# Eight experts written out one by one in a mixture-of-experts stage, with the splitting of their weights shared out over three engines

## The chip, the cores and the metric

One core of one Trainium2 chip. The metric is the device time of one execution in microseconds; engines are TensorE (PE in the profile, its weight loads PEld), VectorE (DVE), ScalarE (ACT), GpSimd (POOL) and SyncE (SP, which here only issues DMAs). T stands for the start of a tile's first matmul where a schedule is worked out.

## The reference, cut to what matters

`x` is 2 x 1024 tokens of 256 features. Two attention layers and a small MLP over the context come first and don't change. Then a top-1 mixture of experts, with 8 experts and a hidden size of 1024:

```python
x = x + _L1_ffn_ref(_layernorm(x), w_router, w1, b1, w2, b2)
# in it:
probs = softmax(x @ w_router); sel = argmax(probs); wgt = probs[sel]
for e in range(8):
    h = relu(xt @ w1[e] + b1[e])          # 256 -> 1024
    y = h @ w2[e] + b2[e]                 # 1024 -> 256
    out = out + ((sel == e) * wgt)[:, None] * y
```

## The kernel before

The program is a row of blocks with a barrier of all engines between them. The last two matter here: `context_mlp` (span 451 to 531 us), which ends with the routing, and `experts` (531 us to the end).

**Routing.** `context_mlp` normalises the rows, computes the router's logits, and gives each token a slot: the tokens of an expert fill tiles of 128 slots, and each expert's first slot starts a new tile. `steps` decides how many tiles an expert has: its first entry is -1, so that an expert has at least one tile, even with no token. `MT` = 23 is the most tiles there can be; how many there are (`TILES`) is known only on the chip. `table` holds for each tile its expert, then for each tile whether it exists, then where each expert's tiles end. Rows go to DRAM (`rows`, with mean and 1/std beside them), and POOL fetches the rows of a tile by an indirect DMA (`gather`) to `xg`.

**Weights.** Matmuls run in fp32r. For precision each fp32 operand is split into a rounded high part and the rest: `wh` and `wl` for weights, `xh`/`xl` and `hh`/`hl` for the two layers' inputs, and each product is three matmuls (high x high, low x high, high x low). Raw weights of an expert (`wst`, 2 MB with both layers) and a bias row come by DMA from SP; all three have two buffers, by `e % 2`. Experts 0 and 1 are fetched in `context_mlp`. There ACT makes the high parts of both (8 copies, L1234), and POOL the low parts of expert 0 (`low(0)` to `low(3)`, L1662); the low parts of expert 1 are POOL's at the start of `experts`. For every later expert POOL makes both parts, in three pairs (L1501 high, L1504 low: two halves of the first layer at 1024 columns, then the second layer at 2048), when the first tile of the expert before it begins. SP fetches an expert's weights when the low parts of expert e-2 are done (`next_expert`).

**A tile.** `tiles` runs `body(0)` and then a loop on every engine over the tiles from 1 to `TILES`, with the tile's expert read from `table` into a register and all weight and bias addresses computed from it. In the order of each queue, for tile g:
- PE: `hidden(g)` (L1615, 12 matmuls of 512 columns), `transpose_x(g+1)` (L1604), `output(g-1)` (L1634, 24 matmuls of 256 columns), `transpose_h(g)` (L1624, 8 transposes).
- DVE: `e_h` (L1583, bias added, two halves), `x_low(g+1)` (L1562), `finish(g-1)` (L1568 `e_y`, then L1571, which adds the weighted result to the row in `xg`), `e_hl` (L1591, two halves), `normalise(g+2)` (L1557).
- ACT: `x_high(g+1)` (L1536), relu to `e_hh` (L1545, two halves).
- POOL, written out for every g up to `MT` with conditions from `table`: gather of tile g+3 (L1668), the next expert's split where a new expert begins, and the scatter of tile g-1 to the output (L1527). Reads of `table` into registers are at L1471.

`e_y` of tile g is computed while tile g+1 is under way, and PE's `output(g)` stands behind `hidden(g+1)` in its queue.

Of the kernel before, what the change touches and what calls it, by code (L numbers as in the profile page):

```python
# [10 lines left out]
ALU = mybir.AluOpType  # L11
# [26 lines left out]
ROW = D + 2  # L38
MT = B * S // P + NE - 1
TG = MT + 2  # L40
TABLE = 2 * TG + NE + 1
TILES, LAST = 2 * TG + NE - 1, 2 * TG + NE
# [1069 lines left out]
def context_mlp(nc, top, t, io):  # L1112


    with ExitStack() as ctx:
# [3 lines left out]
        def sem(name):  # L1119
# [7 lines left out]
        mv4, rstd4 = x_all[:, :, D:D + 2], x_all[:, :, D + 1]  # L1127
# [21 lines left out]
        w_high = t["w_high"] = sem("c_w_high")  # L1149
# [11 lines left out]
                 "inner_s", "th_s", "g_s", "o_ps", "x_done", "r_ps", "shift", "exp", "oh_s", "count_ps", "sent_s", "here_s", "inv_ps", "src_s")  # L1161
        (dve, pool_sem, consts, var_ready, rstd_ready, xn_ready, xT_ps, xT_sb, h_ps, sq_ready, inner_ready,
         th_ready, g_ready, o_ps, x_done, r_ps, shifted, exp_done, oh_ready, count_ps, sent_ready, here_ready, inv_ps, src_ready) = (
# [3 lines left out]
        @block.sync  # L1167
        def _(sp):
            fetch_expert(sp, t, io, 0)
            sp.wait_ge(t["w_in"], 48)  # L1170
            fetch_expert(sp, t, io, 1)
            rows = t["rows"].rearrange("(t p) r -> p t r", p=P)
            for n in range(NC):
                sp.wait_ge(rstd_ready, n + 1)
                sp.dma_start(rows[:, n * CH:(n + 1) * CH], x_all[:, n * CH:(n + 1) * CH]).then_inc(stored, 16)
            next_expert(sp, t, io, 2)

        @block.gpsimd
        def _(pool):
# [18 lines left out]
            def low(i):  # L1198
                split_low(pool, t, w_high, i)

            power(0)
            low(0)
            power(1)
            low(1)
            power(2)
            power(3)
            low(2)
            low(3)
# [5 lines left out]
        def _(act):  # L1214
# [15 lines left out]
            def high(i):  # L1230
                x, q = divmod(i, NC)
                act.wait_ge(t["w_in"], 48 * (x + 1))
                part = quarter(q)
                act.copy(t["wh"][:, x, part], t["wst"][:, x, part]).then_inc(w_high, 1)  # L1234

# [4 lines left out]
            for n in range(1, NC):  # L1240
# [3 lines left out]
                if n >= 2:  # L1244
                    high(n - 2)
            copy_x(NC + 1)
            high(2)
            copy_x(NC + 2)
            high(3)
            copy_x(NC + 3)  # L1250
            high(4)
            high(5)
            act.wait_ge(shifted, 1)
            act.activation(e[:], e[:], ACT.Exp).then_inc(exp_done, 1)
            high(6)
            high(7)

        @block.vector
        def _(vec):
            link = Link(vec, dve)  # L1260

            def normalise(i):
# [10 lines left out]
                ins.then_inc(xn_ready, 1)  # L1273

# [35 lines left out]
            vec.memset(steps[:, 0:1], -1.0)  # L1310
# [123 lines left out]
def experts(nc, top, t, io):  # L1434

    with ExitStack() as ctx:
# [3 lines left out]
        def sem(name):  # L1440
# [3 lines left out]
        bias = t["bias"]  # L1444
# [5 lines left out]
        dst, share, landed = t["dst"], t["share"], t["landed"]  # L1450
# [4 lines left out]
        names = ("dve", "xn_s", "xT_ps", "xh_s", "xl_s", "h_ps", "h_sb", "hT_ps", "hh_s", "hl_s",  # L1455
                 "y_ps", "y_s", "y_done", "out_s", "hgone")
        (dve, xn_ready, xT_ps, xh_ready, xl_ready, h_ps, h_sb, hT_ps, hh_ready, hl_ready, y_ps, y_sb,
         y_done, out_done, hgone) = (sem("e_" + n) for n in names)
        w_high = [sem(f"e_w_high{i}") for i in range(3)]
        w_in, w1_ready, w_ready = t["w_in"], t["w1_ready"], t["w_ready"]  # L1460
# [9 lines left out]
        def load(eng, at, top_value, least=0):  # L1470
            return eng.value_load(table[0:1, bass.ds(at, 1)], min_val=least, max_val=top_value)  # L1471

        def tiles(eng, body):

            body(0)
            with eng.Fori(1, load(eng, TILES, MT, NE)) as g:
                body(g)

        @block.sync
        def _(sp):  # L1480
            for e in range(3, NE):
                next_expert(sp, t, io, e)
            written = sp.to_reg(load(sp, TILES, MT, NE) * 16)
# [4 lines left out]
        def _(pool):  # L1488
            most = pool.to_reg(B * S - 1)

            def split(g, e, par):
                fetched = pool.to_reg(e * 48 + 96)
                pool.wait_ge(h_ps, 2 * g)
                pool.wait_ge(w_in, fetched)
                for part in range(3):
                    raw, high, low = (
# [265 lines left out]
```

## Time and profile before

| | us |
|---|---|
| median of 3 runs | 744.81 |
| the three runs | 745.09, 744.81, 739.28 |
| the profiled execution: its time | 744.16 |
| its span in the trace | 742.4 |
| mean granted TensorE clock over the span | 0.895 of full |
| PE, DVE, ACT, POOL busy | 599.1, 498.7, 292.4, 321.5 |

The span is what the trace covers; the 1.76 us between it and the execution's time lie around it. Busy time is summed over the whole program, of which the experts stage is the last 211 us. A granted clock of 1.0 is 2.4 GHz and 0.5 is 1.2 GHz. In a row, "x12" is the number of instructions, and a bracket at the end says how long the engine sat idle before it and what released it.

### The profile page before, as it was taken

The numbers are of one execution on the slowest core, as the hardware profiler recorded it, in microseconds if no ns is written. First come the engines' busy times: TensorE is split into PE (matmuls) and PEld (weight loads), VectorE is DVE, ScalarE is ACT, GpSimd is POOL, SyncE is SP. The second block draws the span as 40 slices with busy tenths as digits, with TensorE's granted clock in tenths as the row PEclk, the third lists the DMA queues.
The fourth block names the chain that finished last, engine by engine and source line by source line (L and its number), as shares of the span: only waits on it lengthen the run. The fifth ranks groups of instructions, "written<-read, shape, count | busy, mean of one in ns | idle before, by whom it ended". The sixth has DMA issues, their size and how long they took to land. (4 is left out here: it accounts for less than half of the span.)

```text
span 742.4 us, 12123 instructions
## 1 busy us (share of the span) xinstructions
PE 599.1 (81%) x3667; PEld 521.3 (70%) x3668; DVE 498.7 (67%) x950; ACT 292.4 (39%) x536; POOL 321.5 (43%) x271
## 2 busy tenths in 40 slices
PE   4588999953579999999999985675668959687984
PEld 4467888953468888888888872465557847576874
DVE  4698888855027888889889864774376636536562
ACT  1144554512146878778788701332012102111210
POOL 3344434421413344344344311250166956697265
PEclk9799999995699999999999997955579989988997
DMA  6111111100344232322322005323032451422110
GB/s 211 29 45 42 30 28 29 29 9 0 90 112 86 47 81 44 83 47 57 72 45 43 0 1 193 134 87 149 20 121 73 156 182 36 174 101 84 43 28 18
DMA packets 24823, 53.10 MB, mean 72 GB/s; under 512 B 4570, under 2 KB 11483, under 8 KB 22730
## 3 DMA queue, kind: packets, MB, share of 16 engines
q1 hardware_dynamic: 20474, 45.10, 20.6%
q0 software_dynamic: 2208, 5.41, 2.6%
q10 hardware_dynamic: 2096, 2.05, 0.9%
q8 instruction: 21, 0.34, 0.2%
q14 instruction: 24, 0.20, 0.1%
HBM read 31.55 MB, written 4.87 MB: 49 GB/s over the span
## 5 line engine op out<-in xcount | busy, mean ns | idle before, releaser
L881 POOL TENSOR_SCALAR h_p<-h_p,h_rs 128x1024 f32<-128x1024 f32 x64 | 72.5, 1132 | 131.5 <-DVE h_rs L973 131.5
L980 DVE TENSOR_REDUCE h_nmx<-h_psS 128x1 f32<-128x1024 f32 x64 | 78.1, 1221 | 22.4 <-PE h_psS L1071 21.0
L960 DVE TENSOR_TENSOR h_pTl<-h_psT,h_pTh 128x512 fp32r<-128x512 f32 x128 | 81.5, 678 | 4.4 <-ACT h_pTh L908 4.4
L908 ACT CAST h_pTh<-h_psT 128x512 fp32r<-128x512 f32 x128 | 69.2, 590 | 29.6 <-PE h_psT L1031 29.6
L930 ACT ACTIVATE h_p<-h_psS,h_nmx 128x1024 f32<-128x1024 f32 x64 | 72.3, 1129 | 17.7 <-DVE h_nmx L980 17.7
L1042 PE MATMUL h_psO<-h_pTh,h_vs 128*128 128x256 f32 x256 | 70.0, 307 | 3.1 <-DVE h_oT L968 2.3
L308 POOL TENSOR_TENSOR a_p<-a_p,a_rs 128x616 f32<-128x616 f32 x32 | 39.0, 1220 | 73.9 <-DVE a_rs L355 73.9
L1031 PE MATMUL h_psT<-ident,h_p 128*128 128x128 f32 x512 | 67.4, 273 | 1.4 <-DVE h_pTl L960 1.2
L1031 PEld LDWEIGHTS h_psT<-ident,h_p 128*128 128x128 f32 x512 | 59.1, 141 | 11.2 <-issue 3.3
L1042 PE MATMUL h_psO<-h_pTl,h_vs 128*128 128x256 f32 x256 | 63.8, 282 | 0.0
L1504 POOL TENSOR_TENSOR wl<-wst,wh 128x1024 fp32r<-128x1024 f32 (+1 forms) x18 | 56.0, 3114 | 2.7
L1071 PE MATMUL h_psS<-h_kh,h_qs 128*128 128x512 f32 x128 | 56.0, 438 | 0.7 <-DMA h_kl<-h_lo 0.7
L1536 ACT CAST e_xh<-e_psX 128x256 fp32r<-128x256 f32 x22 | 8.2, 374 | 119.3 <-PE e_psX L1604 119.3
L1615 PE MATMUL e_psH<-wh,e_xh 128*128 (+1 forms) x84 | 37.8, 450 | 21.4 <-POOL wl L1504 12.5
L1634 PE MATMUL e_psY<-wh,e_hh 128*128 (+1 forms) x168 | 52.7, 314 | 2.5 <-DVE e_hl L1591 2.5
L1042 PEld LDWEIGHTS h_psO<-h_pTh,h_vs 128*128 128x128 f32 x256 | 48.5, 190 | 7.2 <-issue 5.6
L1071 PE MATMUL h_psS<-h_kl,h_qs 128*128 128x512 f32 x128 | 50.9, 397 | 0.0
L1634 PE MATMUL e_psY<-wh,e_hl 128*128 (+1 forms) x168 | 50.4, 300 | 0.0
L1634 PE MATMUL e_psY<-wl,e_hh 128*128 (+1 forms) x168 | 50.3, 299 | 0.0
L1668 POOL DMA_INDIRECT xg<-rows,src x25 | 26.0, 1038 | 54.6 <-DVE src L1352 27.0
L1042 PEld LDWEIGHTS h_psO<-h_pTl,h_vs 128*128 128x128 f32 x256 | 48.8, 191 | 0.3
L1545 ACT ACTIVATE e_hh<-e_psT 128x512 fp32r<-128x512 f32 x42 | 22.9, 595 | 63.8 <-PE e_psT L1624 63.6
(262 smaller groups left out, 1506.3 us busy)
## 6 DMA issues: line engine op xcount, KB each, us to landing
wst<-in_m_w SPq DMA_DIRECT2D x16, 1024.0 KB, 5.9
bias<-in_m_b SPq DMA_DIRECT2D x8, 640.0 KB, 8.6
h_kh<-h_hi SPq DMA_DIRECT2D x32, 128.0 KB, 2.4
h_kl<-h_lo SPq DMA_DIRECT2D x32, 128.0 KB, 2.4
rows<-x_all SPq DMA_DIRECT2D x4, 516.0 KB, 3.4
a_qs<-a_qhi SPq DMA_DIRECT2D x16, 128.0 KB, 2.3
a_qs<-a_qlo SPq DMA_DIRECT2D x16, 128.0 KB, 2.3
h_qs<-h_hi SPq DMA_DIRECT2D x16, 128.0 KB, 2.2
```

The lines of the kernel that those rows point to most:

```text
L308: pool.tensor_tensor(p3, p3, rs[:, u, :].unsqueeze(2).to_broadcast([P, HH, L]), ALU.mult).then_inc(pn_ready, 1)
L881: pool.tensor_scalar(pr[:, u % 4], pr[:, u % 4], rs[:, u:u + 1], 0.0, ALU.mult, ALU.add).then_inc(pn_ready, 1)
L908: act.copy(pTh[u // QP % 2][:, hf * HK:(hf + 1) * HK, u % QP * P:(u % QP + 1) * P], psT[hf][:]).then_inc(pT_hi, 1)
L930: act.activation(pr[:, u % 4], psS[u % 2][:], ACT.Exp, bias=nmx[:, u:u + 1], scale=1.0, accum_out=sm[:, u:u + 1]).then_inc(exp_done, 1)
L960: vec.tensor_tensor(pTl[u // QP % 2][part], psT[hf][:], pTh[u // QP % 2][part], ALU.subtract).then_inc(pT_lo, 1)
L980: vec.tensor_reduce(nmx[:, u:u + 1], psS[u % 2][:], AX.X, ALU.max, negate=True).then_inc(max_ready, 1)
L1031: ins = pe.transpose(psT[hf][:, k], pr[:, u % 4, (hf * HK + k) * P:(hf * HK + k + 1) * P], ident[:])
L1042: ins = pe.matmul(psO[:, 0:QP * P], vs[i % 2][:, k], part[g % 2][:, k], start=(k == 0 and part is pTh), stop=(k == KT - 1 and part is pTl))
L1071: ins = pe.matmul(psS[u % 2][:, hf * CW:(hf + 1) * CW], qs[i % 2][:, q * P:(q + 1) * P], part[i % 2][:, hf * CW:(hf + 1) * CW], start=(par ...
L1504: pool.tensor_tensor(low, raw, high, ALU.subtract).then_inc((w1_ready, w1_ready, w_ready)[part], 1)
L1615: ins = pe.matmul(psH[hf][:], x_[:, k], w_[:].rearrange("p a w -> p (a w)")[:, bass.ds(off, 512)], start=(k == 0 and n == 0), stop=(k == K ...
L1634: ins = pe.matmul(psY[:, 0:D], h_[:, k], w_[:].rearrange("p a w -> p (a w)")[:, bass.ds(off, D)], start=(k == 0 and n == 0), stop=(k == FB ...
```

## The change

- `steps` gets a second entry of -1: every expert has at least two tiles. `MT` becomes 30, `TG` 32.
- `tiles` is written out for the 8 experts: for each a `body` for its first tile and a loop over its others, whose ends are read from `table`. Weight and bias addresses are constants; only the tile's number is a register.
- ACT makes all high parts, in an expert's first tile: the second layer's of this expert (`high2`, two copies) before `x_high(g+1)`, and the first layer's of the next expert (`split_high`, two copies) after it. DVE makes the second layer's low parts of this expert (two subtractions of 1024 columns) between `x_low(g+1)` and `finish(g-1)`. POOL makes the first layer's low parts of the next expert (two subtractions of 1024 columns).
- In `context_mlp` only the first layer of expert 0 is split. SP fetches first-layer weights with the biases, and second-layer weights, apart from each other.
- `normalise` moves from DVE to ACT, as an activation with a scale and a bias per row; `rows` carries -mean/std for it as a third extra column (`ROW` = 259), four small DVE instructions in `context_mlp`.
- Rows are fetched 4 tiles ahead; POOL's gather moves behind the split and into the condition that the tile exists.
- PE waits for both halves of `h_sb` and of `hl` where it waited for one.

The diff, cut to its core:

```diff
-MT = B * S // P + NE - 1
+MT = B * S // P + 2 * (NE - 1)
...
-            vec.memset(steps[:, 0:1], -1.0)
+            vec.memset(steps[:, 0:2], -1.0)
...
             power(0)
-            low(0)
+            split_low(pool, t, 0, 0)
             power(1)
-            low(1)
+            split_low(pool, t, 0, 1)
             power(2)
             power(3)
-            low(2)
-            low(3)
...
         def tiles(eng, body):
-            body(0)
-            with eng.Fori(1, load(eng, TILES, MT, NE)) as g:
-                body(g)
+            for e in range(NE):
+                first = load(eng, ENDS + e - 1, MT - 2 * (NE - e), 2 * e) if e else 0
+                body(first, e, True)
+                with eng.Fori(first + 1, load(eng, ENDS + e, MT - 2 * (NE - 1 - e), 2 * e + 2)) as g:
+                    body(g, e, False)
...
         def _(sp):
-            for e in range(3, NE):
-                next_expert(sp, t, io, e)
+            for e in range(2, NE):
+                sp.wait_ge(low1, 2 * (e - 1))
+                if e >= NB:
+                    sp.wait_ge(bias_free, e - NB + 1)
+                fetch_first(sp, t, io, e)
+                sp.wait_ge(low2, 2 * (e - 1))
+                fetch_second(sp, t, io, e)
...
+            def split(e, par):
+                for hf in range(2):
                     pool.wait_ge(landed, 16)
+                    pool.wait_ge(high1, pool.to_reg(e * 2 + (hf + 3)))
+                    raw, high, low = (halves(w, 1 - par)[:, :, hf] for w in (wst, wh, wl))
+                    pool.tensor_tensor(low, raw, high, ALU.subtract).then_inc(low1, 1)
...
                 with pool.If(load(pool, TG + g - 1, MT) > g - 1):
+                    if g + 4 < TG:
+                        pool.wait_ge(landed, 16 * (g + 4))
+                        gather(pool, t, g + 4)
                     pool.wait_ge(y_done, g)
...
         def _(act):
+            def normalise(g):
+                upto(act, xT_ps, g, 1, 0)
+                upto(act, landed, g, 16, 16)
+                row = xg[:, bass.ds(g, 1), :].rearrange("p a r -> p (a r)")
+                act.activation(xn[:], row[:, 0:D], ACT.Identity, bias=row[:, D + 2:D + 3],
+                               scale=row[:, D + 1:D + 2]).then_inc(xn_ready, 1)
...
+            def body(g, e, first):
+                if first:
+                    for x in range(2):
+                        act.wait_ge(t["in2"][e % 2], 16 * (e // 2 + 1))
+                        act.copy(second(wh, e, x), second(wst, e, x)).then_inc(high2, 1)
                 x_high(g + 1)
+                normalise(g + 2)
+                if first and e + 1 < NE:
+                    split_high(act, t, e + 1, 0)
+                    split_high(act, t, e + 1, 1)
...
         def _(vec):
...
                 x_low(g + 1)
-                if not isinstance(g, int):
-                    finish(g - 1)
+                if first:
+                    for x in range(2):
+                        vec.wait_ge(high2, 2 * e + x + 1)
+                        vec.tensor_tensor(second(wl, e, x), second(wst, e, x), second(wh, e, x),
+                                          ALU.subtract).then_inc(low2, 1)
+                if not first:
+                    finish(g - 1, e)
+                elif e:
+                    finish(g - 1, e - 1)
+                    vec.sem_inc(bias_free, 1)
```

## Rows read from the trace of the kernel before

**Rows 1.** One line's instructions: how often, ns min/median/max, first and last start

```profile
L1568 DVE TENSOR_TENSOR e_y<-e_psY,bias x21: 424/425/426, 556.6 to 735.1; 128x256 f32<-128x256 f32 x21
```

**Rows 2.** Who waited for whom, 530 to 742.4 us: us in total, times, longest

```profile
PE e_psX L1604 <- DVE e_xn L1557: 20.0, 5, 7.7
...
DVE e_xn L1557 <- DMA xg<-rows,src: 12.6, 4, 7.5
```

**Rows 3.** Timeline of POOL, the first instruction of each split; then all scatters of one line

```profile
567.47 1.05 POOL L1501 TENSOR_SCALAR wh<-wst 128x1024 fp32r<-128x1024 f32 x1 [0.47 <-PE e_psH L1615]
...
583.85 1.06 POOL L1501 TENSOR_SCALAR wh<-wst 128x1024 fp32r<-128x1024 f32 x1
...
623.66 1.05 POOL L1501 TENSOR_SCALAR wh<-wst 128x1024 fp32r<-128x1024 f32 x1 [0.40 <-PE e_psH L1615]
...
648.20 1.05 POOL L1501 TENSOR_SCALAR wh<-wst 128x1024 fp32r<-128x1024 f32 x1 [1.06 <-issue]
...
664.45 1.07 POOL L1501 TENSOR_SCALAR wh<-wst 128x1024 fp32r<-128x1024 f32 x1
...
715.00 1.05 POOL L1501 TENSOR_SCALAR wh<-wst 128x1024 fp32r<-128x1024 f32 x1 [0.45 <-PE e_psH L1615]
...
L1527 POOL DMA_INDIRECT out<-xg,dst x21: 1006/1012/1052, 558.0 to 736.6; - x21
```

**Rows 4.** Timeline of all engines, one tile without a split

```profile
556.98 0.48 PE L1615 MATMUL e_psH<-wh,e_xh 128*128 x1
...
559.99 0.36 PE L1634 MATMUL e_psY<-wh,e_hh 128*128 x1
...
560.35 0.37 ACT L1536 CAST e_xh<-e_psX 128x256 fp32r<-128x256 f32 x1 [2.44 <-PE e_psX L1604]
...
562.88 1.04 PE L1624 MATMUL e_psT<-ident,e_h 128*128 128x128 f32 x8
563.28 0.42 DVE L1568 TENSOR_TENSOR e_y<-e_psY,bias 128x256 f32<-128x256 f32 x1 [1.93 <-PE e_psY L1634]
...
564.28 1.28 DVE L1591 SCALAR_TENSOR_TENSOR e_hl<-e_psT,e_hh 128x512 fp32r<-128x512 f32 x2
...
564.40 0.49 PE L1615 MATMUL e_psH<-wh,e_xh 128*128 x1 [0.48 <-issue]
```

**Rows 5.** Timeline around the last split in context_mlp

```profile
496.15 5.45 DVE L1271 TENSOR_SCALAR xg<-x_all 128x256 f32<-128x256 f32 x4 [1.12 <-POOL x_all L1195]
...
501.65 1.97 PE L1376 MATMUL c_psX<-ident,xg 128*128 128x128 f32 x8 [2.44 <-DVE xg L1271]
```

**Rows 6.** Timeline of the first tiles in experts

```profile
540.93 9.30 POOL L1662 TENSOR_TENSOR wl<-wst,wh 128x1024 fp32r<-128x1024 f32 x4
541.62 8.77 DVE L1557 TENSOR_SCALAR e_xn<-xg 128x256 f32<-128x256 f32 x1
542.64 0.28 PEld L1615 LDWEIGHTS e_psH<-wh,e_xh 128*128 128x128 f32 x1 [2.53 <-issue]
```

**Rows 7.** The row update in DVE, and the nearest instructions for the new ones

```profile
L1571 DVE SCALAR_TENSOR_TENSOR xg<-e_y,share,xg x21: 483/1030/2379, 557.2 to 735.7; 128x256 f32 x21
...
L1234 ACT CAST wh<-wst x8: 1027/1043/1049, 475.7 to 513.3; 128x1024 fp32r<-128x1024 f32 x8
...
L1286 DVE SCALAR_TENSOR_TENSOR x_all<-c_psO,x_all 128x1024 f32<-128x1024 f32 x4 | 4.9, 1216 | 0.0
```

**Rows 8.** Timeline of PE: idle times and the matmuls behind them

```profile
574.73 0.49 PE L1615 MATMUL e_psH<-wh,e_xh 128*128 x1 [1.56 <-POOL wl L1504]
...
683.41 0.69 PE L1604 MATMUL e_psX<-ident,e_xn 128*128 128x128 f32 x2 [3.41 <-DVE e_xn L1557]
689.14 1.12 PE L1624 MATMUL e_psT<-ident,e_h 128*128 128x128 f32 x8
...
730.30 0.58 PE L1634 MATMUL e_psY<-wh,e_hh 128*128 128x256 f32 x1 [2.46 <-DVE e_hl L1591]
```

**Rows 9.** Reads of the table into registers by POOL's sequencer

```profile
L1471 POOLq TENSOR_LOAD <-table x70: 282/289/508, 543.3 to 737.7; - x70
```

More of the change, by code:

```diff
@@ L1638, in _, with body, halves, second @@
             transpose_x(0)
-            def body(g):
-                e = 0 if isinstance(g, int) else load(pe, g, NE - 1)
-                before = 0 if isinstance(g, int) else load(pe, g - 1, NE - 1)
+            def body(g, e, first):
                 hidden(g, e)
                 transpose_x(g + 1)
-                if not isinstance(g, int):
-                    output(g - 1, before)
+                if not first:
+                    output(g - 1, e)
+                elif e:
+                    output(g - 1, e - 1)
                 transpose_h(g)
             tiles(pe, body)
-            output(load(pe, LAST, MT - 1, NE - 1), NE - 1)
-def quarter(q):
-    return slice(q * WE // NC, (q + 1) * WE // NC)
-def split_low(pool, t, w_high, i):
-    x, q = divmod(i, NC)
-    part = quarter(q)
-    pool.wait_ge(w_high, i + 1)
-    pool.tensor_tensor(t["wl"][:, x, part], t["wst"][:, x, part], t["wh"][:, x, part],
-                       ALU.subtract).then_inc(t[("w_split", "w1_ready", "w_split", "w_ready")[q]], 2 if q == 1 else 1)
+            output(load(pe, LAST, MT - 1, 2 * NE - 1), NE - 1)
+def halves(w, par):
+    return w[:, par, 0:KD * FF].rearrange("p (k h f) -> p k h f", k=KD, h=2)
+def second(w, e, x):
+    half = FB * D // 2
+    return w[:, e % 2, KD * FF + x * half:KD * FF + (x + 1) * half]
+def split_high(act, t, e, hf):
+    act.wait_ge(t["in1"][e % 2], 32 * (e // 2 + 1))
+    act.copy(halves(t["wh"], e % 2)[:, :, hf], halves(t["wst"], e % 2)[:, :, hf]).then_inc(t["high1"], 1)
+def split_low(pool, t, e, hf):
+    pool.wait_ge(t["high1"], 2 * e + hf + 1)
+    pool.tensor_tensor(halves(t["wl"], e % 2)[:, :, hf], halves(t["wst"], e % 2)[:, :, hf],
+                       halves(t["wh"], e % 2)[:, :, hf], ALU.subtract).then_inc(t["low1"], 1)
 def gather(pool, t, g):
@@ L1696, in program @@
         t["src"], t["dst"], t["share"] = sb("src", [P, TG], I32), sb("dst", [P, TG], I32), sb("share", [P, TG])
-        for name in ("c_in", "w_in", "w1_ready", "w_ready", "w_split"):
+        for name in ("c_in", "high1", "low1", "high2", "low2"):
             t[name] = top.enter_context(nc.semaphore(name))
+        for name in ("in1", "in2"):
+            t[name] = [top.enter_context(nc.semaphore(f"{name}_{i}")) for i in range(2)]
         t["rows"] = nc.dram_tensor("rows", (B * S, ROW), F32, kind="Internal").ap()
```

152 lines of the change are left out of this document (59 added, 93 removed).

## The prediction

> **What bounds the kernel now.** I read the stage from its ends inward. First, one line that every tile runs once: `e_y` ran 21 times, from 556.6 to 735.1 us [rows 1], so the stage had 21 tiles, the first result came at 556.6, and the other 20 took 178.5 us, 8.9 each. Second, a tile in which nothing goes wrong [rows 4]: PE goes from `hidden` at 556.98 to the next `hidden` at 564.40, 7.42 us. The reader is to see in it that `hidden` and the transposes of x take 3.01, `output` 2.89 (559.99 to 562.88), and the transposes of h 1.04, which makes 6.94 of work, and somewhat less in truth, since the ends are modelled: the two `e_y` at 556.6 and 563.28 [rows 1, 4] are 6.7 apart. I call it 6.8. The last row says that 0.48 before the next tile was "issue", PE waiting for its own sequencer (branch, two reads of the table, address registers). So PE is the bound of a quiet tile, and 8.9 - 6.8 is what the rest costs. Third, the waits [rows 2]: PE waited 20.0 us for the normalised row, and DVE, which normalises, 12.6 for gathered rows; at other places PE waited for POOL's low weights (1.56 at 574.73 [rows 8] is one). All three go back to POOL, which splits the weights of experts 2 to 7 and is late with its gathers for that. The starts of the splits [rows 3] also give the tiles of each expert: a split begins with the first tile of experts 1 to 6, and POOL's 21 scatters (558.0 to 736.6, the last of these rows), counted between those starts, give 3, 1, 5, 2, 1, 7, 1, 1. Four experts have one tile.
>
> **What the change takes away.** (a) In `context_mlp` four normalising instructions took 5.45 us while POOL ran two low parts, and PE waited 2.44 for them [rows 5]. POOL has nothing to run there now: -2.4. Tables of 32 instead of 25 entries lengthen seven small DVE instructions on the same path by some 0.1 each: +0.8. Together **-1.6**. ACT's copies there were idle time and gain nothing.
> (b) At the start of `experts` one `e_xn` took 8.77 us beside four of POOL's subtractions, and PE had its next `hidden` at 542.64 after 2.53 of "issue" [rows 6]. After the change `hidden(1)` can start near 541 and takes 5.1 at half clock (12 matmuls of 512 columns); low part work for expert 1 hides behind ACT's copies; `hidden(1)` and the transposes of x end near 546.4, where before `e_xn` held them until 541.62 + 8.77 = 550.4; `output(0)` at full clock and the 0.4 to `e_y` make 549.6 of the 556.6 of [rows 1]: **-7.0**. It would be 2.4 less if the clock were still low then.
> (c) The waits of [rows 2] are gone as such: POOL keeps two subtractions of six instructions an expert, `normalise` is no longer on the engine that stalls beside POOL's subtractions, and gathers, 4 ahead, lead by three tiles (some 20 us). The longest wait for a gathered row was 7.5, well inside that; if the lead were lost, the 12.6 of [rows 2] is what it costs. They don't enter the sum, which counts what an interval takes after the change.
>
> **What it adds: tiles.** A minimum of two tiles turns the four single ones into two: 25 tiles, 24 intervals instead of 20. A tile inside a loop has no table read and no address work in PE's queue, so I take 6.85, the 6.8 of work and little else (bounds 6.8 and the 7.42 of [rows 4]). The first tile of an expert and the step into its loop still have one read each: 7.1. With 15 such steps and 9 plain ones: 15 x 7.1 + 9 x 6.85 = 168.2.
>
> **What it adds: a collision.** Take a first tile with T at PE's `hidden`, with the offsets of [rows 4]. ACT copies `high2` at T+0.2 to 2.3 (two of 1.04 [rows 7]), hidden. `x_high` is at T+3.4 to 3.75, `normalise` to 4.2 (no row has it; the bounds are the 0.37 for rounding the same size from PSUM [rows 4] and the 1.04 for four times the size [rows 7], and I take 0.45, near the first), `split_high` to 5.2 and 6.2, all before the relu at 6.6. DVE ends `x_low` near 4.25 and makes two low parts of 1.15 to 1.2 each (no row has a subtraction of this size on DVE; the nearest is 1.22 for 1024 columns [rows 7]): until 6.55. POOL starts its first low part when ACT's first half is there, 5.4, or when DVE lets go, 6.55; a pair takes 4.7 (four took 9.30 [rows 6]), so it holds until 10.1 to 11.3. In this time stands `finish(g-1)`, whose second instruction reads two operands from SBUF: it takes 0.48 alone and up to 2.38 beside POOL [rows 7]. And `e_xn` shows that a waiting DVE doesn't get in between two of POOL's subtractions that stand back to back: 8.77 us over four [rows 6]. So the row update, due at T+6.9, ends at 11.6 (if DVE's second part came first) or 12.2 (if POOL came first), `e_hl` behind it at 12.8 to 13.4, and PE, which wants it for `output(g)` at T+7.1+3.0 = 10.1, waits 2.7 to 3.3. The cover that DVE had, `e_hl` ending 1.6 before its use, is used up. Experts 1 to 6 have it (0 has no `finish` there, 7 no next expert): 6 x 2.9 = **17.4**. Bound below: 0.7 each if DVE gets in after one subtraction.
>
> **And the clock.** After 1.56 us of idle PE's matmuls ran at full speed (0.49 for 512 columns), after 2.46 and 3.41 at half (0.58, 0.69) [rows 8]. Behind the second, transposes of x and `output` took 5.73 (683.41 to 689.14) instead of some 3.1, so +2.6; behind the first, `output` took 4.4 (from 730.30 to 0.4 before the last `e_y` at 735.1 [rows 1]) instead of 2.89, so +1.5. Idle times of 2.7 to 3.3 fall on the wrong side: 1.9 each, as the smaller of the two is the nearer, and eight tenths of the six, 11.4: **9.1**. Bounds 0 and 6 x 2.6 = 15.6.
>
> **The end.** POOL walks through the tiles that don't exist: 2 before, 5 now, with six more reads of the table, each about 0.6 with its register work (0.29 alone [rows 9]). They come after the last scatter. If the core's end waits for POOL's last step all of it counts (+3.6), if for the scatter's completion nothing: **+2.0**.
>
> Sum on the profiled execution, whose span is 742.4: -1.6 - 7.0 + (168.2 + 17.4 + 9.1 - 178.5 = +16.2) + 2.0 = 752.0, with the 1.8 around it **753.8** (744.16 before, which is 0.65 under the median). Without collision and clock it would be 727: the gain of the freed PE pays for four more tiles and leaves 17 us, and the collision is what spends it.
>
> **Rivals.** *The clock stays up* (a gap of 2.7 is nearer to 2.46 than to 3.41, and what ran before 730.30 was itself interrupted): 744.7, no change. *DVE gets in after the first subtraction*: for it, no row update took over 2.38 [rows 7] though POOL's passes from [rows 3] are six instructions long, so DVE did get in where a subtraction was followed by a rounding copy; against it, both places with subtractions back to back [rows 5, 6] held DVE to the end. Its price is 0.7 a time and no clock loss: 753.8 - 26.5 + 4.2 = **731.5**, faster. It decides from whether the row update ends below T+9.
>
> By the Trainium skill, "SBUF — State Buffer", section "SBUF: two separate sides", the port pair is a lock that whichever starts first has for the whole of one instruction, which makes this rival the expected course; by that rule the time would be this rival's 731.5, and the 8.77 us of [rows 6] should have been some 2, which the trace contradicts. The same page says that two SBUF inputs make a DVE instruction contend, so that DVE's own low parts take part in it.
>
> *Entering loops is dear*: the one step into the loop that the trace has cost PE 2.53 us of "issue" at its weight loads [rows 6], against 0.48 between tiles [rows 4]. Eight entries and seven exits at 2.0 more each would be 30; six fall into the wait of the collision, so 18: **772**. Against it: three reads of the table stood in that step, and only one is left.
>
> The Trainium skill, "Runtime: NRT & Kernel Launch", section "Instruction fetch mechanics", says that a branch to code outside the two pages held forces a fetch; eight loops instead of one would give that more chances, which is this rival's case. The trace of before doesn't separate it from the table reads.
>
> **How the numbers follow.** Collision with the clock loss 0.50; clock stays up 0.17; DVE gets in 0.22; dear loops 0.11. The first by itself runs from 746 to 760 (collision 2.7 to 3.3, clock 1.5 to 2.4, end 0 to 3.6). For 8 in 10 the range takes in all of these but half of the dear loops and the lower half of the fast rival's spread: 729 to 766. A change of 1% (737.4 and 752.3 against the median) is what can be told from none here. Faster: the fast rival, 0.22. Slower: two thirds of the first and the last, 0.44. Within: the rest, 0.34.
>
> **What would show it.** `e_y` x25, the first near 548. Quiet intervals of 6.8 to 7.1. In the first tiles of experts 1 to 6 the row update (`finish`) near 4 us or DVE's second low part that long, then PE idle 2.5 to 3.5 for `e_hl` ahead of `output`, and its matmuls at half speed. Right before: no `e_xn` wait, no wait for `wl`. It would be wrong if the stage's first tiles are as short as its others (fast rival), if "issue" before PE's matmuls grows (dear loops), or if gathers or weights come late in spite of (c), for which I have no term.

## The result: slower, 774.5 us

The changed kernel takes 774.5 us (median of 4 runs, 768.2 to 775.5) against 744.95 in the runs beside it, a ratio of 1.040 (95% interval 1.036 to 1.044). Forecast were 753.8 and a range of 729 to 766. The profiled execution has a span of 772.9 against 742.4, so 30.5 us have to be found. Here and below ratios rest on the fast runs alone, those within 1.5% of a kernel's fastest, while medians and ranges take in all runs.

**First the same line as before.** Tile results (`e_y`) and row updates of the kernel after, one line's instructions (how often, ns min/median/max, first and last start):

```profile
L1568 DVE TENSOR_TENSOR e_y<-e_psY,bias x25: 415/424/426, 555.2 to 750.5; 128x256 f32<-128x256 f32 x25
L1570 DVE SCALAR_TENSOR_TENSOR xg<-e_y,share,xg x25: 484/486/2699, 555.9 to 751.1; 128x256 f32 x25
```

Set against [rows 1], there are 25 tiles, as forecast; the first comes 1.4 us earlier, and the 24 intervals take 195.3 instead of 178.5. After the last `e_y` 22.4 us are left, where it was 7.3. The stage's first `e_xn` starts at 536.65 instead of 531.22. So the 30.5 are: context stage and routing +5.4 (0.9 of it arises ahead of the stage, in code that is the same: its first instruction starts at 451.75 instead of 450.88); from there to the first `e_y` -6.8; intervals +16.8; last `e_y` to last scatter +7.1 (8.5 in place of 1.4); last scatter to the end +8.1 (13.9 in place of 5.8).

**Then the waits.** Kernel after, 528 to 773 us (in total, times, longest; the rows that matter here):

```profile
POOL xg L1680 <- issue: 84.3, 24, 7.9
ACT e_xn L1530 <- DMA xg<-rows,src: 52.7, 17, 9.2
PE e_psY L1637 <- DVE e_hl L1596: 11.9, 8, 2.8
PE e_psX L1608 <- ACT e_xn L1530: 9.7, 3, 5.4
PE e_psH L1618 <- POOL wl L1493: 7.3, 4, 3.0
POOL out L1519 <- issue: 7.3, 24, 0.3
```

The wait of `normalise` for gathered rows, 12.6 in [rows 2] and declared gone by my part (c), is now 52.7, in 17 places. And POOL waits for no finished tile any more: before each scatter it sits idle for only 0.3. The scatters start 4.1 to 16.1 us after the row update that they wait for has ended. POOL is the engine that is late.

**What POOL does in a tile.** Timelines of POOL, then of ACT's `normalise`, in a stretch without a split:

```profile
611.37 1.02 POOL L1680 DMA_INDIRECT xg<-rows,src  x1 [7.13 <-issue]
612.69 1.02 POOL L1519 DMA_INDIRECT out<-xg,dst  x1 [0.30 <-issue]
617.11 1.03 POOL L1680 DMA_INDIRECT xg<-rows,src  x1 [3.40 <-issue]
618.44 1.03 POOL L1519 DMA_INDIRECT out<-xg,dst  x1 [0.30 <-issue]
623.22 1.02 POOL L1680 DMA_INDIRECT xg<-rows,src  x1 [3.76 <-issue]
624.55 1.02 POOL L1519 DMA_INDIRECT out<-xg,dst  x1 [0.30 <-issue]
629.87 1.02 POOL L1680 DMA_INDIRECT xg<-rows,src  x1 [4.29 <-issue]
```

```profile
608.71 0.60 ACT L1530 ACTIVATE e_xn<-xg 128x256 f32 x1 [8.22 <-DMA xg<-rows,src]
614.46 0.60 ACT L1530 ACTIVATE e_xn<-xg 128x256 f32 x1 [3.92 <-DMA xg<-rows,src]
620.27 0.60 ACT L1530 ACTIVATE e_xn<-xg 128x256 f32 x1
```

A quiet pass takes 5.7 to 6.7 us from gather to gather: until the gather has landed (2.84 the first time, and the scatter stands inside this time), then three reads of the table with their register work (0.6 to 0.7 each), then 0.7 before the next gather goes out. The row gathered at 611.37 is normalised at 614.46, as soon as it lands, and behind the gather of 617.11 the same 3 us follow. In the whole stage no row is normalised more than 7.6 us after its gather went out. Rows are asked for "4 ahead", yet no lead is left. The reason is a line of the change that my list of it left out, though it is part of the diff, behind each scatter:

```
 pool.indirect_dma_start(out=io["out"], ..., in_=xg[:, g - 1, 0:D], ...).then_inc(out_done, 16)
+pool.wait_ge(landed, 16 * min(g + 5, TG))
```

`gather(g + 4)` is the (g + 5)th, so POOL stands in each pass until the gather that it has just issued has landed. Before, it waited for the gather of the pass before, which had landed beside the wait for the tile. A pass with a split (two subtractions of 4.7 to 4.9 more, and waits around them) takes 10.2 to 12.4. The passes right behind the first four splits are nearly as long, 9.5 to 10.2: the end of a split lets SP fetch another expert's first-layer weights, and the gather that goes out in the same moment lands only after 6.6 (issued at 601.87, landed at 608.46), with POOL waiting for it. TensorE's tile is 6.7 to 7.0, so a quiet pass wins back 1 us at best, and the two passes around such a split lose 6 or more. There was no lead to begin with: gathers 3 and 4 stand behind the split of expert 1, and the first scatter starts 10.8 us after its row update. Even through six quiet tiles on end POOL stays 6.5 to 7.2 behind.

Six of the 24 intervals are over 10 us. Three have a late row in them, the other three POOL's late low parts: PE waited 3.03, 1.99 and 1.83 for these and went on at a granted clock of 0.50 to 0.66. One of each kind:

```profile
609.37 0.44 PE L1608 MATMUL e_psX<-ident,e_xn 128*128 128x128 f32 x2 [1.86 <-ACT e_xn L1530]
...
639.91 0.79 PE L1618 MATMUL e_psH<-wh,e_xh 128*128 128x512 f32 x1 [3.03 <-POOL wl L1493]
```

The chain that ended last, from the profile's page, says the same of the whole execution:

```profile
DMA xg<-rows,src 15%; POOLq L1455 4%; POOL wl L1493 2%; POOL wl L1674 0%; POOL out L1519 0%; POOL xg L1680 0%; POOLq L1514 0%; POOLq L1508 0%; ACT wh L1668 0%; POOLq L1506 0%; POOLq L1680 0%; POOLq L1511 0%; POOLq L1491 0%; ACT e_xn L1530 0%; ACTq L1455 0%
```

15% of 772.9 is 116 us in which the end hung on a gathered row: nothing that an engine computes. Before it was 5%.

**The context stage.** Timeline of DVE, then of POOL, kernel after; these answer to [rows 5]:

```profile
477.37 1.37 DVE L1253 TENSOR_SCALAR xg<-x_all 128x256 f32<-128x256 f32 x4
478.66 2.31 DVE L1258 SCALAR_TENSOR_TENSOR x_all<-x_all 128x4 f32<-128x4 f32 x1
480.89 1.21 DVE L1272 SCALAR_TENSOR_TENSOR x_all<-c_psO,x_all 128x1024 f32<-128x1024 f32 x1
...
491.21 2.31 DVE L1258 SCALAR_TENSOR_TENSOR x_all<-x_all 128x4 f32<-128x4 f32 x1
```

```profile
477.75 3.20 POOL L1674 TENSOR_TENSOR wl<-wst,wh 128x1024 fp32r<-128x1024 f32 x1 [2.32 <-ACT wh L1668]
484.24 1.11 POOL L1194 TENSOR_TENSOR x_all<-x_all,c_mhalf 128x4 f32<-128x4 f32 x1 [3.29 <-DVE x_all L1276]
490.29 3.21 POOL L1674 TENSOR_TENSOR wl<-wst,wh 128x1024 fp32r<-128x1024 f32 x1 [4.94 <-ACT wh L1668]
```

The new shift of four columns, -mean/std, reads two operands from SBUF, and two of the four took 2.31 us, until POOL's low part ended, with the update of `x_all` queued behind them (the other two, with POOL quiet, took 0.16). I had no term for these instructions at all.

**The end.** Reads of the table by POOL from 755 us on, and its last step before the end:

```profile
L1455 POOLq TENSOR_LOAD <-table x11: 283/288/293, 755.3 to 767.5; - x11
...
L1422 POOLq DRAIN  x1: 4484/4484/4484, 768.2 to 768.2; - x1
```

The last scatter, at 759.0, is followed by the wait for a gather, the reads of five tiles that don't exist until 768.2, and a drain of 4.5.

### The profile page after: what moved, and what is told of

It reads as the page before. It is cut to its first block and busy times, and to the rows that moved or that the text cites. A ratio compares the mean times of both kernels' runs of the same rounds, so it can differ in the third digit from the quotient of the medians.

```text
span 772.9 us, 11969 instructions
## 1 busy us (share of the span) xinstructions
PE 626.2 (81%) x3851; PEld 548.7 (71%) x3851; DVE 510.4 (66%) x974; ACT 336.1 (43%) x599; POOL 272.0 (35%) x252
## 5 line engine op out<-in xcount | busy, mean ns | idle before, releaser
L1680 POOL DMA_INDIRECT xg<-rows,src x30 | 32.1, 1069 | 132.4 <-issue 84.3
L1637 PE MATMUL e_psY<-wh,e_hh 128*128 128x256 f32 x200 | 61.2, 306 | 12.0 <-DVE e_hl L1596 11.9
L1637 PE MATMUL e_psY<-wh,e_hl 128*128 128x256 f32 x200 | 58.8, 294 | 0.0
L1637 PE MATMUL e_psY<-wl,e_hh 128*128 128x256 f32 x200 | 58.8, 294 | 0.0
L1618 PE MATMUL e_psH<-wh,e_xh 128*128 128x512 f32 x100 | 44.9, 449 | 9.5 <-POOL wl L1493 7.3
L1581 DVE TENSOR_TENSOR e_h<-e_psH,bias 128x512 f32<-128x512 f32 x50 | 33.7, 688 | 25.5 <-PE e_psH L1618 23.7
L1637 PEld LDWEIGHTS e_psY<-wh,e_hh 128*128 128x128 f32 x200 | 40.4, 202 | 14.1 <-DVE e_hl L1596 14.1
L1530 ACT ACTIVATE e_xn<-xg 128x256 f32 (+1 forms) x27 | 16.2, 602 | 72.5 <-DMA xg<-rows,src 52.7
```

The lines of the kernel that those rows point to most:

```text
L1581: vec.tensor_tensor(h[:, hf], psH[hf][:], b1(e, hf), ALU.add).then_inc(h_sb, 1)
L1618: ins = pe.matmul(psH[hf][:], x_[:, k], halves(w_, e % 2)[:, k, hf], start=(k == 0 and n == 0), stop=(k == KD - 1 and n == 2))
L1637: ins = pe.matmul(psY[:, 0:D], h_[:, k], w_[:, e % 2, at:at + D], start=(k == 0 and n == 0), stop=(k == FB - 1 and n == 2))
```

## The experiments

Each ratio is to the kernel before, run beside it on the same chip; the kernel before has medians of 740.7 to 744.95 on the different chips, so medians of different chips can differ by 4 us for that alone. e1 to e4 share a chip, so do e6 to e9, and e10 to e12.

```
run                   us median (range)        ratio [95%]              tiles  intervals  last scatter to end
after                 774.5 (768.2 to 775.5)   1.040 [1.036, 1.044]     25     195.3      13.9
e1_no_landed          741.4 (733.3 to 750.4)   0.997 [0.994, 1.001]     25     181.8      11.2
e2_shift_last         766.0 (763.2 to 768.2)   1.033 [1.028, 1.038]     25     194.2      14.0
e3_short_tail         756.3 (755.9 to 758.4)   1.020 [1.016, 1.023]     25     185.3       8.4
e4_three              729.5 (725.1 to 732.7)   0.982 [0.976, 0.988]     25     174.1       5.8
e5_before_two_tiles   784.9 (784.0 to 786.2)   1.057 [1.053, 1.060]     25     207.4      18.6
e6_gathers_first      718.3 (711.7 to 725.9)   0.961 [0.956, 0.966]     25     168.3       5.7
e7_split_late         726.4 (725.3 to 727.5)   0.978 [0.974, 0.981]     25     169.9       6.2
e8_all                718.2 (714.6 to 719.0)   0.967 [0.964, 0.971]     25     162.3       6.2
e9_single             711.7 (708.4 to 714.3)   0.958 [0.953, 0.963]     21     158.7       5.2
e10_single_early      701.3 (697.4 to 704.3)   0.945 [0.939, 0.951]     21     147.9       5.0
e11_pieces            722.1 (719.1 to 723.7)   0.974 [0.969, 0.978]     25     164.7       7.8
e12_pieces_single     702.6 (700.4 to 705.6)   0.947 [0.941, 0.952]     21     152.9       5.0
```

**One repair at a time, and together.** First the wait alone:

```
-                    pool.wait_ge(landed, 16 * min(g + 5, TG))
```

> The changed kernel without the one wait that POOL has behind every scatter, for the landing of the gather it has just issued (the gather's own wait for its predecessor stays). Theory A, POOL's serial chain (gather 1.0, landing 2.8 to 7.3, table reads, and the split behind it) is what made rows late (ACT waited 52.7 us for them) and left POOL 8.5 us behind the last row update: 24 intervals shrink from 195.3 to 172 to 185 us and the lag at the end by some 7, so 746 to 760 us. Theory B, as predicted blind, the collision of POOL's subtractions with DVE's row update is the price: the gathers come earlier, nothing else moves, 768 to 776. Theory C, gathers are late because weights are being fetched, not for the order in POOL: half of A's gain, 760 to 768.

Measured: 0.997, 4.3% or some 32 us less than the change, more than any of the three expectations, and level with the kernel before. Waits of e1, 528 to 748 us:

```profile
POOL xg L1679 <- DMA xg<-rows,src: 45.4, 14, 6.3
POOL out L1519 <- DVE xg L1569: 28.8, 11, 3.2
ACT e_xn L1529 <- DMA xg<-rows,src: 18.9, 5, 9.5
```

POOL waits for finished tiles again (28.8, where it was next to nothing), and its scatters start 0.3 to 6.0 us after their row updates, but for the first (10.8). `normalise` waits for rows in 5 places instead of 17, four of them among the first tiles. The trace is of an execution of 750.4 us, 9 above the median, so its parts add to 24 only: intervals 13.5, the lag behind the last `e_y` 7.1, the end 2.7, the first `e_y` 0.9. Theory C has a share in the mechanism: a gather beside a fetch of weights still takes 6.6 to land here, only nothing stands still for it any more. This one line is the difference between a change that costs 30 us and one that costs nothing.

Second, the shift in one instruction of 16 columns after the last `normalise`, with one wait for it in SP:

```
-                if i >= NC:
-                    part = slice(n * CH, (n + 1) * CH)
-                    vec.scalar_tensor_tensor(shift4[:, part], mv4[:, part, 0], ...).then_inc(shift_ready, 1)
+                if i == 2 * NC - 1:
+                    vec.scalar_tensor_tensor(shift4, mv4[:, :, 0], ...).then_inc(shift_ready, 1)
```

> The changed kernel with the four 128x4 instructions that make -mean/std in context_mlp put into one 128x16 behind the last normalising, so that the four stores of rows wait for it. Theory A, two of the four (2.31 us each where 0.16 is the bare cost) stood behind POOL's subtractions and delayed the stage: the stage is 4.3 us shorter, 769 to 771 us. Rival, the delay was hidden by PE or the stores become late instead (they take 4 us each and the first gather waits for them at 532): 773 to 776.

Measured: 766.0 us, less than was expected, and the first `e_y` at 546.3, 9.0 earlier; the new instruction, no longer beside POOL, takes 0.18:

```profile
L1257 DVE SCALAR_TENSOR_TENSOR x_all<-x_all x1: 183/183/183, 495.8 to 495.8; 128x16 f32<-128x16 f32 x1
```

Of the 9.0, 2.0 arise ahead of the stage, in code that is the same (its first instruction starts at 449.76 instead of 451.75). So the shifts cost 7.0: 4.3 are the two holds, and 2.6 a wait of DVE for ACT's tanh behind the first (4.11 instead of 1.49). Without them the stage gained 2.5 on the kernel before, where I forecast 1.6. In the ratio 0.7% came of it (some 5 us).

Third, POOL's conditions for tiles 17 on nested in each other, so that the first tile that doesn't exist skips the rest; tiles 1 to 16, which always exist, lose their condition and its table read:

```
-                with pool.If(load(pool, TG + g - 1, MT) > g - 1):
+            for g in range(1, 2 * NE + 1):
+                tile(g)
+            with ExitStack() as rest:
+                for g in range(2 * NE + 1, MT + 1):
+                    rest.enter_context(pool.If(load(pool, TG + g - 1, MT) > g - 1))
+                    tile(g)
```

> The changed kernel with POOL's conditions for tiles 17 to 30 nested in each other, so that after the last live tile it reads the table once instead of nine times. Theory A, the core's end waits for POOL's last step and then its drain: 9.2 us from the last scatter to the drain become 2.5 to 3, so 767 to 769 us. Rival, the drain waits for the last scatter's own completion (it took 4.5 us after the dead tiles): the drain grows by what the steps lose, 772 to 775.

Measured: 2.0% less than the change (15 us, twice what was expected). The end took 8.4 in place of 13.9; the rest came in the intervals, 185.3 in place of 195.3. The landed wait is still in this kernel, and one table read less (0.29 in each pass, and what goes with it) paid because POOL's pass set the pace. POOL's drain stayed as it was (4.56, 4.48 in the change), so the rival is out.

> All three edits together. If they are independent (theory A each): 774.5 less 14 to 28, less 4.3, less 6.5, so 736 to 750 us. If the collision that was predicted blind only appears once POOL is on time (its subtractions then begin at T+5.4 to 6.5 of an expert's first tile and the row update stands at T+6.9), the trace shows row updates of 4 to 5 us for experts 1 to 6, PE idle of 2.5 to 3.5 behind each, and the time is at the upper end or over it, 745 to 755.

All three together: 0.982, 1.8% faster than before, and 729.5 us is under both expectations. The gains alone add to 4.3 + 0.7 + 2.0 = 7.0 points, together they give 5.8; the first and the third shorten the same passes, though with the intervals of the four ratios the difference isn't far from noise. What is left shows in the intervals: 22 of 24 are 5.6 to 7.8, and two are 11.6 and 12.1.

**The price of the tiles by itself.** The kernel before with only the minimum of two:

```
-MT = B * S // P + NE - 1
+MT = B * S // P + 2 * (NE - 1)
-            vec.memset(steps[:, 0:1], -1.0)
+            vec.memset(steps[:, 0:2], -1.0)
```

> The kernel before with only the minimum of two tiles for each expert (25 tiles in place of 21; nothing else of the change). It prices the added tiles alone. Theory: four more intervals of about 7 us, and fewer weight stalls since experts of one tile are gone (the two intervals of 17 us of before shrink): 24 intervals of 186 to 200 us against 178.5, total 10 to 26 us slower, ratio 1.014 to 1.035. Rival, by which the tiles cost their whole count and nothing is given back: 4 x 8.9 = 36 us slower, ratio 1.048. Rival, by which the old stalls were worth the added tiles: within 5 us, ratio 0.995 to 1.007.

Measured: +5.7%, 42 us, above all three expectations. Timeline of POOL at its end:

```profile
765.84 1.01 POOL L1527 DMA_INDIRECT out<-xg,dst  x1 [3.35 <-DVE xg L1571]
767.15 1.02 POOL L1668 DMA_INDIRECT xg<-rows,src  x1 [0.31 <-issue]
771.53 1.00 POOL L1668 DMA_INDIRECT xg<-rows,src  x1 [3.36 <-DMA xg<-rows,src]
775.93 1.00 POOL L1668 DMA_INDIRECT xg<-rows,src  x1 [3.40 <-DMA xg<-rows,src]
```

28.9 are the intervals, 7.2 a tile that was added. 12.7 are the end: the old loop gathers outside the condition, and 25 tiles with room for 30 leave three gathers of rows of tiles that don't exist, 4.4 each, behind the last scatter. The changed kernel has its gathers inside the condition. So the minimum of two costs the old kernel 42, of which the changed one has only the tiles to pay; how its 30 split into tiles and the rest can't be had by subtracting the two.

**The first tiles.** e4 had one interval of 11.6, with ACT 9.6 in wait for a row until 553.3: gather 3 was queued behind POOL's subtractions for expert 1, and POOL had waited 5.8 for gather 1, beside a weight fetch. e6 is e4 with

```
-            for g in range(1, 3):
+            for g in range(1, 5):
                 pool.wait_ge(landed, 16 * g)
                 gather(pool, t, g)
             split_low(pool, t, 1, 0)
             split_low(pool, t, 1, 1)
-            for g in range(3, 5): ...
```

and the fetch of expert 2's first layer at the end of `context_mlp` instead of at the start of `experts`.

> The kernel with all three repairs (e4), plus gathers 1 to 4 issued ahead of POOL's subtraction pair for expert 1, and the fetch of expert 2's first layer issued at the end of the context stage instead of at the experts' start. Theory: the first tiles of e4 waited for rows only because gather 1 took 5.1 us beside that fetch and gather 3 was issued behind the subtractions of 4.7 us (ACT's normalise waited 9.6 us for it). Then the first interval falls from 11.6 to about 7.2, gather 1 lands in 3 us, and the kernel is 3 to 8 us faster than e4: ratio 0.971 to 0.978 against e4's 0.982. Rival: the four gathers in a row push expert 1's low parts behind the point where TensorE wants them, and the stall only moves to interval 2 or 3: no gain, ratio 0.980 to 0.984.

Measured: 0.961, more than expected (2.2 points under e4, though the ratio rests on few runs and the range is wide). The first interval is 6.8, the first `e_y` at 544.1 (548.9 in e4): the theory held, the rival didn't.

**The collision of my forecast.** In e4 it is there once, whole. Timelines of DVE, POOL and PE:

```profile
581.41 0.42 DVE L1570 TENSOR_TENSOR e_y<-e_psY,bias 128x256 f32<-128x256 f32 x1
582.02 5.58 DVE L1572 SCALAR_TENSOR_TENSOR xg<-e_y,share,xg 128x256 f32 x1 [0.19 <-DVE e_y L1570]
587.52 1.27 DVE L1598 SCALAR_TENSOR_TENSOR e_hl<-e_psT,e_hh 128x512 fp32r<-128x512 f32 x2
...
593.49 0.42 DVE L1570 TENSOR_TENSOR e_y<-e_psY,bias 128x256 f32<-128x256 f32 x1 [3.17 <-PE e_psY L1639]
```

```profile
581.56 1.02 POOL L1516 DMA_INDIRECT out<-xg,dst  x1 [0.30 <-issue]
582.60 4.71 POOL L1492 TENSOR_TENSOR wl<-wst,wh 128x1024 fp32r<-128x1024 f32 x2
```

```profile
588.85 0.39 PE L1639 MATMUL e_psY<-wh,e_hh 128*128 128x256 f32 x1 [3.85 <-DVE e_hl L1598]
```

The row update is held through both subtractions, `e_hl` stands behind it, PE idles 3.85 us, and `output` then takes 4.6 to `e_y` (588.85 to 593.49). In e6 it came once too, in another place; PE idled 3.74, `output` took 4.66 from 626.99 to 631.65, and the granted clock of that stretch was 0.72 of full speed:

```profile
core 0: us, PE busy (x) PEld busy (x) DVE busy (x) ACT busy (x) POOL busy (x), PEclk, DMA share, GB/s
...
619.00:626.00 7.00, 4.25 (x26) 3.44 (x24) 6.80 (x4) 2.49 (x5) 6.82 (x4) 1.00 0.56 187
626.00:632.00 6.00, 5.01 (x30) 5.01 (x31) 2.81 (x6) 0.00 (x0) 1.68 (x2) 0.72 0.86 326
```

e7 is e4 with the two subtractions moved behind the scatter, which waits for the row update (so the gather, too, goes out ahead of them):

```
+                pool.indirect_dma_start(out=io["out"], ...).then_inc(out_done, 16)
                 if g < MT:
                     e = load(pool, g, NE - 1)
                     ... split(e, par)
-                pool.indirect_dma_start(out=io["out"], ...).then_inc(out_done, 16)
```

> The kernel with all three repairs (e4), plus POOL's two subtractions of an expert moved behind the scatter of the same pass, so that they start after VectorE's row update has been made. Theory (my forecast's own collision): the one interval of 12.1 in e4 with its row update of 5.58 us comes from the update falling beside POOL's pair and from the clock lost after it; it goes to about 7.0, and no row update is longer than 2.4: 4 to 6 us faster than e4, ratio 0.974 to 0.977. Rival: the collision moves to another VectorE operation (a low part, 2.35 us the pair) or the late low parts hold TensorE or the next fetch: same as e4 or up to 6 us slower, ratio 0.981 to 0.990.

Measured: no row update over 2.61, and behind the first interval (13.2 here, 11.6 in e4) none over 8.9, so 24 take 169.9 instead of 174.1. The ratio, 0.978, is lower than e4's 0.982, but the intervals overlap: the mechanism is shown in the trace, its price in the time isn't told from none.

> The changes of e6 and of e7 together. If both theories hold the gains add, as they lie in different intervals: 718 to 723 on the scale on which e4 ran 729.5, ratio 0.966 to 0.973, 24 intervals of 163 to 166 us. If one of the two only moves its stall, it shows here as in that run.

Measured: 0.967, and the fewest us for 24 intervals, 162.3, 6.8 each. But it isn't under e6: the medians are the same (718.2 and 718.3), and the intervals of the ratios overlap. The collision is rare enough in e6 that removing it doesn't show in the time.

In e11 each subtraction of e6 is four:

```
-                    pool.tensor_tensor(low, raw, high, ALU.subtract).then_inc(low1, 1)
+                    for k in range(KD):
+                        for c in range(2):
+                            cut = slice(c * 256, (c + 1) * 256)
+                            ins = pool.tensor_tensor(low[:, k, cut], raw[:, k, cut], high[:, k, cut], ALU.subtract)
+                    ins.then_inc(low1, 1)
```

> The kernel of e6 with each of POOL's two subtractions of 128x1024 written as four of 128x256, at the same place. Theory: VectorE is let in between two POOL instructions, and what holds its row update is one instruction's length (2.36 us for a whole one); then no row update is longer than about 1.3 us, the interval of 11.9 is gone and 24 intervals take 163 to 165 in place of 168.3. Total 0 to 6 us less than e6: ratio 0.953 to 0.962. Rival, by which POOL once started keeps VectorE out until it pauses: with no pause between the pieces a row update of 5 us and an interval of 12 still appear, and POOL's pieces cost 0.1 to 0.3 us more each: ratio 0.960 to 0.968.

Measured: in the six places no row update took over 1.05 us (the theory said 1.3), and no interval is over 8.5. Yet the kernel isn't faster than e6. By its ratio, 0.974, it is slower, beyond the rival's figure as well; but its range (719.1 to 723.7) lies inside that of e6 (711.7 to 725.9). POOL's eight pieces take 5.61 instead of 4.7 (timeline of POOL and of DVE):

```profile
571.94 1.03 POOL L1520 DMA_INDIRECT out<-xg,dst  x1 [0.30 <-issue]
573.00 5.61 POOL L1498 TENSOR_TENSOR wl<-wst,wh 128x256 fp32r<-128x256 f32 x8
```

```profile
578.12 0.78 DVE L1576 SCALAR_TENSOR_TENSOR xg<-e_y,share,xg 128x256 f32 x1 [0.20 <-DVE e_y L1574]
```

What the pieces do to the hold is shown; whether the kernel is slower for them isn't (the spans of the two traces are 717.3 and 719.5, the other way round, and e6 wasn't run on the chip of e11).

**One tile again.** e9 is e8, and e10 is e6, with a minimum of one tile and each loop behind a branch:

```
-                with eng.Fori(first + 1, load(eng, ENDS + e, ...)) as g:
-                    body(g, e, False)
+                second_ = first + 1
+                last = load(eng, ENDS + e, ...)
+                with eng.If(last > second_):
+                    with eng.Fori(second_, last) as g:
+                        body(g, e, False)
```

> The kernel of e8 with a minimum of one tile for each expert again, each loop behind a branch that skips it where the expert has a single tile (21 tiles in place of 25). Theory: every tile costs a full interval of 6.7 to 7.0 whatever rows it holds, so four fewer give 26 to 28 us less than e8: ratio 0.930 to 0.937, near 692 to 697. Rival: experts of a single tile leave no quiet interval to round and split the next weights in, so the stalls of weights come back (9 to 17 us intervals as in the kernel before), and half of it is given back: ratio 0.945 to 0.955.

> The kernel of e6 (POOL's subtractions ahead of the gather) with a minimum of one tile, as e9 is that of e8. Theory: in e9 each stall of 15 us was TensorE waiting 5 to 7 us for POOL's low part of the first layer, which was queued behind the wait for the finished tile; issued ahead of it they come some 3 us earlier: three intervals of 11 to 12 in place of 15, 6 to 10 us less than e9: ratio 0.945 to 0.950. Rival: a single tile is too short for fetch, ACT's rounding and POOL's subtraction in a row wherever they stand; same stalls, ratio 0.955 to 0.960.

Measured: e9 0.958, only 7 us under e8, above even its rival's figure. Three intervals are 14 to 15.4 (PE, timeline):

```profile
563.93 0.79 PE L1623 MATMUL e_psH<-wh,e_xh 128*128 128x512 f32 x1 [5.42 <-POOL wl L1498]
```

e10, with the subtractions ahead of the gather, has 9.9, 12.1 and 10.8 there and comes to 0.945: 701.3 us, the fastest of all. So the theory of e10 held: half of the stall was the place of the subtractions, the other half stays. In the new order four tiles more cost 1.5% (e6 against e10) by the ratios, 3 us each, and 5 each by the intervals of the two traces (168.3 and 147.9); in the kernel before the intervals grew by 7.2 each (e5).

> e10 with the pieces of e11. If the pieces help (theory of e11), ratio 0.940 to 0.947; if VectorE is kept out by the whole row of pieces, as e10 or 2 us slower.

Measured: 0.947, the same as e10. No update in those places over 1.05 here either, but one weight stall was 15.7 (12.1 in e10). There PE was ready 2.5 us earlier, while POOL's pair started at the same time (617.27, in e10 617.36), so that PE idled 6.10 instead of 3.32 and went on at a granted clock of 0.50. The ratio fits both expectations, so for the time it decides nothing; for the hold it repeats e11.

## Why the prediction was wrong

**The step that failed is (c).** It says that gathers "lead by three tiles (some 20 us)" and that the waits of [rows 2] "don't enter the sum". I derived the lead from the number 4 in the code and not from POOL's pass, and in listing the change I passed over the added wait. The pass could have been worked out: in the trace before gathers land 2.8 to 7.2 us after their issue (median 3.5), reads are 0.29 each [rows 9], and a split is 4.7 (half of the 9.30 of [rows 6]). Landing 3.5 with the scatter inside it, and three reads with their register work at 0.6 each, are 5.3, and with the 0.7 that the trace after shows before each gather, 6.0, for a tile of 6.85: less than 1 us is won back in a pass, and six splits of 4.7, with gathers of up to 7.2 behind them, have to come out of it. The prediction did give a price for a lost lead, 12.6; it was 32 (e1), and 52.7 us of waiting for rows in 17 places stood where it had put none.

**The number by itself.** Of the 20.9 us between the 752.0 of the sum and the span of 772.9, 13.2 stand at the end, 7.0 in the context stage, 0.8 in the rest. That the intervals add nothing to the miss is luck, as the next paragraph shows.

**Point by point.** *First tiles*, -7.0: measured -6.8. *Tiles*, 24 intervals of 168.2 if nothing else stands in the way: e8 162.3, e6 168.3 with one collision in it, so the term was some 6 us dear. *Intervals in sum*, +16.2: measured +16.8, which looks like a hit and isn't. The collision in my figure wasn't there; late rows and late low parts were, and where the clock fell, it fell behind those. In the change only four updates took 2.1 to 2.7 us: as POOL ran late, its pairs fell elsewhere. *Collision*, 6 x 2.9: where the landed wait is gone it came in one or two of six places (12.1 for 7.0, so 5.1 each with the clock, and I had said 4.8 with it). So size and chain were right and the count was wrong. *Clock*: idle of 3.74 and 3.85 cost about 1.3 in `output` (4.6 for the 3.3 of a quiet tile), and I took 1.9. *Context*, -1.6: +5.4, of which 4.6 arise in the stage, because the shifts, worth 7.0, were left out (e2). *End*, +2.0: +15.2 in all, of which 7.1 is POOL's lateness and 8.1 the dead tiles with the gather before them. The bound of +3.6 was too low: from the last scatter's start 2.5 us pass until the first of nine reads (761.5), and these take 0.74 each with the way round each condition.

**The rivals.** *DVE gets in after the first subtraction* was mostly the course of things: see the last section. Its 731.5 is what the ratio of e4 gives on the time before (0.982 x 744.95), which has the change without the three things I had no proper term for; some of that is luck, as e4 has one whole collision. *Dear loops*: in e4 PE's weight loads have one "issue" of that sort, 1.61 at 539.07, and none at any other entry, and quiet intervals are 6.5 to 7.0; out. *The clock stays up*: no, it fell behind 3.7 us of idle. Of the four cases none contained a late POOL, and my closing words, "if gathers or weights come late in spite of (c), for which I have no term", name the case that came.

## What to carry to other kernels

A prefetch distance in the code is no lead: add up the pass of the engine that issues the fetches, with every wait in it, and compare it with the consumer's tile; if the pass isn't clearly shorter, the distance is used up after the first disturbance. Never let a queue wait for the transfer that it has just issued, unless something needs it there: this one line cost 4.3%. And when a sum comes out right in total, compare its parts with the trace before trusting it: here +16.2 met +16.8 for another reason.

## What the runs showed of the hardware

**How long POOL holds DVE depends on where DVE's instruction starts.** All rows are of the row update (0.48 alone, two SBUF operands) beside POOL's pair of subtractions. Timelines of e1, of DVE, then of POOL:

```profile
588.84 5.40 DVE L1569 SCALAR_TENSOR_TENSOR xg<-e_y,share,xg 128x256 f32 x1 [0.19 <-DVE e_y L1567]
628.79 2.02 DVE L1569 SCALAR_TENSOR_TENSOR xg<-e_y,share,xg 128x256 f32 x1 [0.19 <-DVE e_y L1567]
```

```profile
589.24 4.71 POOL L1493 TENSOR_TENSOR wl<-wst,wh 128x1024 fp32r<-128x1024 f32 x2
627.44 5.63 POOL L1493 TENSOR_TENSOR wl<-wst,wh 128x1024 fp32r<-128x1024 f32 x2 [3.84 <-ACT wh L1667]
```

In e1, e4, e6 and e10 all five updates of 5.4 to 5.6 us (two of them in e1) were recorded as started 0.4 to 0.6 *before* the pair, while POOL's scatter was running, and ended with the pair's second subtraction; those of about 2.0 started during the first subtraction and got in before the second, the pair being 5.6 to 5.9 long then. By the Trainium skill, "SBUF — State Buffer", section "SBUF: two separate sides", whichever of the two starts first has the port pair for its whole instruction. The updates of 2.0 and the pieces of e11 and e12 (1.05 at most) agree with a hold of one instruction; the five of 5.4 to 5.6 don't, neither in who comes first nor in how long. Why an early start is the worse one isn't shown.

**An instruction of four columns can cost more than one of a thousand**: 2.31 us for the shift beside POOL's low part, where the same instruction took 0.16 with POOL quiet, and the update of 1024 columns behind it 1.21.

**The end of POOL's program isn't free**: its drain took 3.7 to 4.8 us in all fourteen kernels, 3.75 in the kernel before, 4.48 in the change. It wasn't shorter when the last scatter was longer ago: 4.29 when the drain began 0.5 us after the scatter's start (e10), 4.48 when it began 9.2 after (the change).
